# Order of the products in the first step of each group of the second expert product (attention, routing and mixture of experts on one core)

## The reference, cut to what matters

```python
x = x + xattn(layernorm(x), ctx_512, W_k, b_k, ln_gamma, ln_beta)      # (4, 1024, 1024)
x = x + ffn(layernorm(x), gate_w, w1, w2, w3)

# ffn: E = 8 experts, TOP_K = 2, D = 1024, M = 3584
topk_w, topk_idx = top_k(softmax(x_flat @ gate_w), 2)
x_rep_sort = take(x_flat, sort_idx // 2)                # rows sorted by expert
h = silu(ragged_dot(x_rep_sort, w1, group_sizes)) * ragged_dot(x_rep_sort, w3, group_sizes)
out_sort = ragged_dot(h, w2, group_sizes)               # the second product
out = einsum('tkd,tk->td', unsort(out_sort), topk_w)
```

## Time and profile before

| | |
|---|---|
| Time, median of 3 runs | 7672.02 us (7668.89 to 7682.15) |
| The profiled execution: its own time | 7680.66 us |
| The profiled execution: span from first to last instruction | 7679.2 us |
| PE busy | 7383.2 us, 96% of the span |
| DVE busy | 5059.7 us, 66% |
| ACT busy | 2891.5 us, 38% |
| PE matmuls of the up projections (line 1743) on the chain that ended last | 59% of the span |
| PE matmuls of the second product (line 1776) on that chain | 30% |
| Mean granted clock of TensorE | 0.982 of full speed |

### The profile page before, as it was taken

How to read it: one execution, slowest core, us unless ns; L and a number is a source line. 1 busy time by engine, 2 the same in 40 slices (tenths; PEclk the granted TensorE clock), 3 DMA queues, 4 the chain that set the end, 5 groups by cost and what they waited for, 6 DMA issues and landing times.

```text
span 7679.2 us, 143199 instructions
## 1 busy us (share of the span) xinstructions
PE 7383.2 (96%) x45405; PEld 6551.7 (85%) x45406; DVE 5059.7 (66%) x8017; ACT 2891.5 (38%) x4875; POOL 917.7 (12%) x1347
## 2 busy tenths in 40 slices
PE   8968999999999999999999999999999999999998
PEld 5547887788779999988779999978778999999998
DVE  6767766677656665577656675577666766567655
ACT  2314334433443334433343334433353333433343
POOL 2331010100111001100111001110101001110011
PEclk9879999999999999999999999999999999999999
DMA  3323446544564446544565445544465445644455
GB/s 118 107 96 131 160 155 203 182 155 154 190 205 136 153 144 191 170 160 160 179 190 161 155 148 190 183 153 154 173 195 173 144 159 176 184 156 144 154 191 164
DMA packets 684138, 1247.24 MB, mean 162 GB/s; under 512 B 50560, under 2 KB 286480, under 8 KB 683920
## 3 DMA queue, kind: packets, MB, share of 16 engines
q1 hardware_dynamic: 584240, 935.24, 37.2%
q0 software_dynamic: 99680, 310.10, 12.3%
HBM read 841.86 MB, written 405.38 MB: 162 GB/s over the span
## 4 chain that ended last, share of the span: by engine, by line
PE 90%; DVE 1%; issue 1%; ACT 0%; DMA 0%; POOL 0%; DVEq 0%; ACTq 0%; POOLq 0%
PE pair L1743 59%; PE pair L1776 30%; PE pair L1864 1%; DVE wl L1348 0%; PE pair L1845 0%; DVE sil L1351 0%; DVE sil L1611 0%; DVE xl L1348 0%; DVE hid L1611 0%; DMA part<-x_rows,id_g 0%; ACT wh L1108 0%; POOL out_x L1981 0%; DVE hid L1351 0%; PE pair L1854 0%; ACT part L1108 0%
## 5 line engine op out<-in xcount | busy, mean ns | idle before, releaser
L1743 PE MATMUL pair<-xh,wh 128*128 128x272 f32 (+1 forms) x9408 | 2504.9, 321 | 27.5 <-DVE xl L1348 17.1
L1743 PE MATMUL pair<-xh,wl 128*128 128x272 f32 (+1 forms) x9408 | 2517.9, 322 | 0.0
L1743 PE MATMUL pair<-xl,wh 128*128 128x272 f32 (+1 forms) x9408 | 2517.2, 322 | 0.0
L1348 DVE TENSOR_TENSOR wl<-raw,wh 128x512 fp32r<-128x512 f32 (+1 forms) x1875 | 1276.3, 701 | 937.9 <-ACT wh L1108 936.4
L1743 PEld LDWEIGHTS pair<-xh,wh 128*128 128x128 f32 x9408 | 1558.3, 188 | 172.3 <-issue 29.3
L1743 PEld LDWEIGHTS pair<-xh,wl 128*128 128x128 f32 x9408 | 1556.6, 188 | 137.6
L1743 PEld LDWEIGHTS pair<-xl,wh 128*128 128x128 f32 x9408 | 1553.6, 188 | 140.1
L1108 ACT ACTIVATE wh<-raw 128x512 fp32r<-128x512 f32 (+1 forms) x1875 | 1148.4, 636 | 1368.8 <-PE pair L1743 665.2
L1776 PE MATMUL pair<-wh,wl 128*128 128x272 f32 (+1 forms) x4704 | 1261.4, 322 | 0.0
L1776 PE MATMUL pair<-wl,wh 128*128 128x272 f32 (+1 forms) x4704 | 1260.5, 322 | 0.0
L1776 PE MATMUL pair<-wh 128*128 128x272 f32 (+1 forms) x4704 | 1144.2, 326 | 64.2 <-DVE wl L1348 43.8
(11 more groups left out here) (253 smaller groups left out, 5516.5 us busy)
## 6 DMA issues: line engine op xcount, KB each, us to landing
raw<-in_L_ffn_w SPq DMA_DIRECT2D x226, 1024.0 KB, 7.6
raw<-hd SPq DMA_DIRECT2D x720, 272.0 KB, 3.7
hd<-hid SPq DMA_DIRECT2D x112, 1088.0 KB, 4.4
hd<-sil SPq DMA_DIRECT2D x112, 816.0 KB, 6.8
raw<-w2s SPq DMA_DIRECT2D x256, 256.0 KB, 3.3
w2v<-in_L_ffn_w POOLq DMA_DIRECT2D x113, 512.0 KB, 3.5
xg<-in_L_ffn_w POOLq DMA_DIRECT2D x113, 512.0 KB, 4.3
w2s<-w2v POOLq DMA_DIRECT2D x112, 512.0 KB, 5.1
```

What stands on the lines that cost most here:

```text
L1348: return V.tensor_tensor(out, a, b, ALU.subtract)
L1743: mm = pe.matmul(to[:, c, 0:hi - lo], entry(w, e)[:, ks], x[:, e, k, lo:hi], start=begin and k == 0 and i == 0, stop=k == KH - 1 and i == ...
```

## The change

In the first step of every group the products are done accumulator by accumulator, as in the other steps: hh, hl and lh of accumulator 0, then of accumulator 1, and so on. The number of products, their operands and the place of each semaphore operation relative to its accumulator stay the same. In the group `i3 = 0` the wait for `s_acc[d]` stays in front of the hh product of accumulator d, and so moves with it. The `rest` calls that stood behind the If/Else now stand in each of its two branches, so each of the three widths has these matmuls twice in PE's code.

```diff
                     for d in range(4):
                         pe.wait_ge(s_acc[d], s * EVENTS + 2 + 2 * p)
                         part_of(0, d, wh, wh, begin=True)
+                        rest(0, d, False)
                 with pe.Else():
                     with pe.If(i3 > SHORT):
                         ready(t0 + i3 * 3 - 1)
                     with pe.Else():
                         ready(t0 + i3 * 3)
                     for d in range(4):
-                        part_of(0, d, wh, wh)
-                for d in range(4):
-                    rest(0, d, False)
+                        rest(0, d, True)
                 with pe.If(i3 > SHORT):
                     ready(t0 + i3 * 3)
```

## The result

The changed kernel takes 7713.64 us (median of 5 runs, 7707.31 to 7730.88) against 7672.02 us: ratio 1.0056, 95% interval 1.0039 to 1.0072. It is slower by some 42 us where 7 us less were forecast, and outside the stated range of 7654 to 7680. The profiled execution took 7730.88 us, span 7729.4.

The account below looks back on a forecast made before the run. PE was taken as the bound, busy for 96% of the span. The median 7672.0 us less 7.4 us of waits in first steps, other terms nil or without a mean, gave 7664.6 us; range 7654 to 7680.

Parts of the forecast that it names:

- What bounds the kernel: PE, busy for 96% of the span; only time in which PE waits at the second product can be won.
- what the change removes: In first steps of passes 0, 2, 5 and 6, PE's waits for accumulators 1 to 3 vanish: 7.4 us won.
- (a) to (c): In first steps, the remaining accumulator waits, the moved semaphore rises and the branches cost nothing.
- rival 2: PE waits for DVE's low parts in a pass's later steps, giving the gain back: 7672 us, no change; chance 0.10.
- (d): First steps of groups keep their pace in the new order, 2.72 us narrow: change nil, bounds +10 and -6 us.
- Rival 1: First steps of groups take on the second step's pace: +4 us, 7669 us, or 7675 with narrow alone; chance 0.18.
- (e): At heads of pass 3 the low clock costs up to 2.4 us in each of eight passes: +-4 us, no mean.
- (f): PE's code grows by 40 matmuls and their loads; nothing for it in the sum.
- rival 3: PE's slot code no longer stays loaded: +28 us (7693) if reloaded each slot, +196 (7861) if each pass; chance 0.04.

Follow-up runs that it names:

- run 1: The changed kernel measured again with no edit: 7716.05 us, ratio 1.0053 to the kernel before.
- run 2: The changed kernel with never-run code ahead of PE's slot loop, putting the loop 164 instructions later: 7673.54 us, ratio 0.9989 to the kernel before.
- run 5: The changed kernel with its slot loop shifted 84 instructions later by never-run code: 7708.19 us in a single run.
- run 6: The changed kernel with its slot loop shifted 140 instructions later by never-run code: 7660.68 us in a single run.
- run 8: The same kernel as in run 6, timed: 7665.27 us, ratio 0.999 to the kernel before.
- run 7: The kernel before with the new order in the 512 column form alone, the wide forms keeping the old order: 7672.35 us, ratio 0.9993.
- run 3: The kernel before, old order and loop length, with its slot loop shifted 84 instructions later by never-run code: 7720.02 us, ratio 1.0045.

## Why the prediction was wrong, point by point

**What bounds the kernel, and what the change removes: right.** First steps of passes were to win 7.4 us. They won 6.9 to 7.2 us in the traces of runs 1, 2, 5, 6 and 8 (146.4 us to between 139.2 and 139.5), and the narrow half, 3.6 forecast, 3.5 in run 7. All excess went, also in pass 0.

**(a) to (c), waits, semaphores, branches: right.** The steps behind the first take the same time (2.79 and 2.74 us), and nothing is given back: rival 2 is out.

**(d), the pace of the first step: right.** 2.72 us in the new order for narrow steps. The wide ones of 528 columns take 3.03 us in the mean before and 3.02 after, those of 544 columns 3.04 both times, so they kept their pace too; the 2.96 us of the earlier trace rows was one step and not the mean. Rival 1 is out.

**(e), the clock: half right.** The first steps of the eight passes 3 sum to 38.7 us before and to 34.4 to 39.2 in the other traces, so they moved by up to 4.3 us, about the +-4 given. What was not seen is that a new pause elsewhere would lower the clock too.

**(f) and rival 3: this is the step that failed.** The mechanism was named, with its place and its sign in the trace (more than 14 loads on queue 8, "issue" at heads of slots), and priced at 28 us for one load in each slot. It got a chance of 0.04, no place in the range, and nothing in the sum. The reason given was that nothing in the rows said the limit was near, and that the code fits "in seven blocks both times". The length was right: 1594 and 1674 instructions counted in the compiled list, 1,580 and 1,660 in the prediction. The number of blocks was not: a loop of 1594 or of 1674 instructions touches seven blocks of 256 or eight, by where it begins, and that was never asked. By runs 5 and 6 the next boundary is 85 to 140 instructions behind its beginning; the loop then has room for 85 to 140 + 1536 = 1621 to 1676 instructions up to the end of its seventh block, and needs 1594 before and 1674 after. So 27 to 79 instructions were to spare, and the change added 80. Where the boundaries fall was found by shifting the loop; whether the compiled list alone tells it was not tried. In the prediction's own terms: its point (f), the longer code, was put at nothing because the length fitted in the room; the runs show that the blocks touched decide, and in run 1 the term measured +21 us of pauses and +14 us of low clock.

The Trainium skill (Runtime: NRT & Kernel Launch, Instruction fetch mechanics) states room for 2048 instructions on PE in blocks of 256, which makes eight, and that the next block is fetched while the present one is executed. An estimate from that page: eight blocks of the loop and the one fetched ahead are nine, one more than is held, and seven and one are eight. The runs agree: they show 14 or 15 loads where the loop touches seven blocks and 31 to 52 where it touches eight. The same section also says that a taken branch stops the engine for a load where its target is not in the current window of two pages. With that window every slot would load again, and the runs do not agree: the kernel before has no load on queue 8 behind 1190 us, though its closing branch leads back over the whole loop. No run shows how many blocks are held, nor the fetch ahead, by themselves.

**The size.** One load at 3.5 us for each slot was 28 us. Run 1 shows two loads for each slot, of which only the one at the closing branch costs much: the pause between slots grew from 12.3 to 33.3 us, 3.0 us for each of seven, 21 us. The rest of the loss is from two things that rival 3 did not have. The clock was low behind a stop, which costs some 2 us a slot in the up projections (14 us). And in two of the four traces with reloads a long pause of 8 to 15 us comes, with a row of loads, once in the changed kernel and three times in run 3. What decides whether it comes is open. It fits that the changed kernel's times scatter by 24 us (7707 to 7731) where those of before scatter by 13: the execution at 7731 us had a long stop, that of run 1 at 7708 us had none.

## What to carry to other kernels

A loop on PE of some 1,600 instructions stood at a cliff here, and what decided on which side of it was the number of fixed blocks that the loop touches, not its length alone. Before duplicating code in such a loop, count its instructions in the compiled list; if it falls over, try shifting the loop by code that is never run, which here brought back the 0.6% that was lost. In a trace, compare the number of instruction loads, the time of the branch that closes the loop and the "issue" waits at its head first: they tell it at a glance, while busy shares and the counts of the matmuls read the same.

## What the runs showed of the hardware that was not expected

- Code that is never executed made a kernel 0.45% slower (run 3) and another 0.6% faster (run 2 against run 1).
- A stop for one instruction block was about 3 us of additional pause for PE at a slot's head, and the 2 us that the lower clock cost behind it were two thirds as much again. Another block, loaded ahead of pass 1 of the same slot, cost some 0.2 us.
- The up projection of a slot of 528 columns has two paces. In the chain that ended last of the kernel before (start, us, what) the three such slots are

```profile
4095.71 573.89 PE pair L1743 x4704
...
5853.40 569.98 PE pair L1743 x4704
6751.88 573.90 PE pair L1743 x4704
```

  and in the sixth kernel's

```profile
4092.78 569.99 PE pair L1743 x4704
...
5841.68 569.99 PE pair L1743 x4704
6738.31 569.99 PE pair L1743 x4704
```

  The same 4704 matmuls take 569.98 or 573.90 us, and the choice holds for the whole phase of a slot. With three such slots, up to 12 us of the difference between two executions of one and the same kernel can be of this kind. What decides it was not tried.
